# Norm squares moved from VectorE to ScalarE over two slots, and every second round of V's transposed tiles copied by ScalarE

## The reference, cut to what matters

```python
q = z @ wq @ fcq_w + fcq_b          # attention A: through 64 columns, with biases
k = z @ wk @ fck_w + fck_b
v = z @ wv @ fcv_w + fcv_b
...
qkv = jnp.einsum('bnc,cd->bnd', x, w_qkv)        # attention B: one dense projection
...
scores = q @ k.T / 8;  attn = softmax(scores);  out = (attn @ v) @ w_out + b_out   # 16 heads of 64
...
h = jax.nn.gelu(x @ w1 + b1, approximate=False);  out = h @ w2 + b2                # 4096 wide
```

## Time and profile before

| quantity | value |
|---|---|
| median of the two timed runs | 3740.32 us |
| the two runs | 3833.94 and 3646.69 us |
| the profiled execution, its own time | 3663.36 us |
| its span (first to last instruction, slowest core) | 3662.3 us |
| spans of the eight cores | 3630.1 to 3662.3 us |
| busy: TensorE, ScalarE, VectorE | 2674.0, 1453.9, 1224.7 us |
| mean granted TensorE clock, cores | 0.854 to 0.869 |

### The profile page before, as it was taken

The page is one execution under the profiler, slowest core; times in us unless marked ns, Lnnn a source line. Parts: engine busy times, 40 slices in busy tenths (PEclk is TensorE's granted clock), DMA queues, the critical chain, the costliest instruction groups (busy, mean ns, idle before and its releaser), DMA issues.

```text
span 3662.3 us, 33549 instructions; the slowest of 8 cores (3630.1 to 3662.3 us)
## 1 busy us (share of the span) xinstructions
PE 2674.0 (73%) x10664; PEld 924.1 (25%) x10664; DVE 1224.7 (33%) x1874; ACT 1453.9 (40%) x1496; POOL 64.8 (2%) x122
## 2 busy tenths in 40 slices
PE   5444878587875577989847658786778765789997
PEld 1110222122222233434313212222122222334333
DVE  4554344434444021120253334444343430212200
ACT  2112989488950202112200009892689601021120
POOL 0000000000000000000000000000000000000000
PEclk9655999789988789999967779998899987899788
DMA  3000000000004715133011110001000038151332
GB/s 104 0 0 6 4 4 4 3 3 5 4 9 62 133 24 92 35 58 69 1 18 18 18 23 4 4 5 26 2 5 4 7 50 140 32 92 35 58 69 92
DMA packets 32806, 121.00 MB, mean 33 GB/s; under 512 B 7552, under 2 KB 11648, under 8 KB 22400
## 3 DMA queue, kind: packets, MB, share of 16 engines
q0 software_dynamic: 20832, 97.53, 15.4%
q1 hardware_dynamic: 11808, 21.32, 1.9%
HBM read 203.50 MB, written 8.39 MB: 58 GB/s over the span
## 4 chain that ended last, share of the span: by engine, by line
PE 51%; ACT 17%; DVE 14%; DMA 7%; issue 6%; another core or an unknown queue 2%; DVEq 1%; SPq 0%; ACTq 0%; POOLq 0%; POOL 0%
ACT POOL L430 14%; DMA POOL<-w_h 5%; PE PS_A L619 5%; DVE POOL L138 5%; PE PS_B L619 5%; PE PS_A L589 5%; PE PS_B L589 4%; PE PS_A L369 3%; PE PS_D L619 3%; PE PS_C L444 3%; DVE SCR L138 3%; PE PS_D L444 2%; DVE sstat L138 2%; PE PS_B L369 2%
## 5 line engine op out<-in xcount | busy, mean ns | idle before, releaser
L430 ACT ACTIVATE POOL<-PS_A,ebias 128x1024 bf16<-128x1024 f32 x512 | 571.0, 1115 | 345.3 <-PE PS_A L374 296.2
L430 ACT ACTIVATE POOL<-PS_B,ebias 128x1024 bf16<-128x1024 f32 x512 | 571.3, 1116 | 32.0 <-PE PS_C L448 13.2
L589 PE MATMUL PS_A<-BIG,POOL 128*128 128x512 bf16 x1024 | 260.6, 401 | 146.7 <-DMA POOL<-w_h 139.4
L369 PE MATMUL PS_A<-BIG,POOL 64*128 64x512 bf16 x512 | 198.1, 387 | 94.0 <-ACT POOL L430 89.8
L142 ACT ACT_TABLE_LOAD x16 | 20.5, 1283 | 613.3 <-PE PS_A L589 518.8
L589 PE MATMUL PS_B<-BIG,POOL 128*128 128x512 bf16 x1024 | 252.6, 391 | 0.0
L369 PE MATMUL PS_B<-BIG,POOL 64*128 64x512 bf16 x512 | 197.9, 387 | 70.9 <-ACT POOL L430 68.1
L138 DVE RECIPROCAL PF<-SCR 33x512 f32<-33x512 f32 x64 | 214.1, 3345 | 65.8 <-DMA SCR<-PF 65.8
L444 PE MATMUL PS_C<-POOL 128*65 128x512 bf16 x512 | 214.8, 420 | 0.0
L444 PE MATMUL PS_D<-POOL 128*65 128x512 bf16 x512 | 206.8, 404 | 6.1 <-ACT POOL L430 6.1
L619 PE MATMUL PS_A<-BIG,POOL 128*128 128x512 bf16 x768 | 188.3, 408 | 28.7 <-DVE BIG L138 26.5
(11 more groups left out here) (139 smaller groups left out, 3013.2 us busy)
## 6 DMA issues: line engine op xcount, KB each, us to landing
POOL<-w_h POOLq DMA_DIRECT2D x64, 1024.0 KB, 8.5
POOL<-w_h POOLq DMA_DIRECT2D x2, 8192.0 KB, 55.1
X<-xT SPq DMA_DIRECT2D x8, 1024.0 KB, 23.2
yT<-X SPq DMA_DIRECT2D x8, 1024.0 KB, 12.2
BIG<-POOL SPq DMA_DIRECT2D x64, 64.0 KB, 1.9
POOL<-wqkv_kv POOLq DMA_DIRECT2D x16, 256.0 KB, 4.3
POOL<-wqkv_q POOLq DMA_DIRECT2D x16, 256.0 KB, 3.5
POOL<-fco_h POOLq DMA_DIRECT2D x8, 256.0 KB, 4.3
```

The costliest lines, as they stand in the source:

```text
L369: nc.tensor.matmul(PSx[:, 0:512], lt0, rh0, start=True, stop=True, tile_position=(0, 0))
L430: nc.scalar.activation(psb, PSx[:, :], AF.Exp, bias=ebias[:, c:c + 1], scale=0.125),
L589: tt = nc.tensor.matmul(PSx[:, ucoff:ucoff + 512], wg[:, dc * 512 + j * 128: dc * 512 + j * 128 + 128], BIG2[:, hoff(dc):hoff(dc) + 512], ...
```

## The change

emit_knorm and emit_qnorm2_and_ebias: the squares are made by ScalarE (Square), in two SBUF buffers in turn; their column sums go to PS_D and PS_E in turn; the row maxima stay on VectorE. The square of slice i waits for the matmul of slice i-2, and the matmul of slice i for the square of slice i and the maximum of slice i-2. On entry ScalarE waits once for everything that TensorE and VectorE have been given so far.

emit_vtranspose: the copies of rounds 1 and 3 are made by ScalarE (Identity), those of rounds 0 and 2 by VectorE as before. Round 3 of the transposes therefore waits for ScalarE, round 2 for VectorE.

Nothing is added to or taken from the number of matmuls, maxima, copies or DMAs; 128 squares and 128 tile copies change engine.

```diff
@@ emit_vtranspose
-                    p.wait(nc.tensor, "dve", round_ev[r4 - 2])
+                    p.wait(nc.tensor, round_eng[r4 - 2], round_ev[r4 - 2])
...
-                p.wait(nc.vector, "te", t)
+                if r4 % 2 == 0:
+                    p.wait(nc.vector, "te", t)
+                else:
+                    p.wait(nc.scalar, "te", t)
...
+                    if r4 % 2 == 0:
+                        v = vop("tensor_copy", da, sa)
+                    else:
+                        v = sop("activation", da, sa, AF.Identity)
                 round_ev[r4] = v
+                round_eng[r4] = "dve" if r4 % 2 == 0 else "act"
@@ emit_knorm
+            p.wait(nc.scalar, "te")
+            p.wait(nc.scalar, "dve")
+            psl = [PS_D[0:1, 0:512], PS_E[0:1, 0:512]]
...
-                p.wait(nc.vector, "te")
-                v = vop("tensor_mul", ksq, kc_ap, kc_ap)
-                p.wait(nc.tensor, "dve", v)
-                t = p.inc(nc.tensor.matmul(PS_D[0:1, 0:512], ones_b[:, 0:1], ksq,
-                                           start=True, stop=True), "te", 1)
-                p.wait(nc.vector, "te", t)
-                vop("reduce_max", S_KSL(sl), PS_D[0:1, 0:512], axis=AX.X)
+                if sl >= 2:
+                    p.wait(nc.scalar, "te", tmm[sl - 2])
+                sq = sop("activation", ksq, kc_ap, AF.Square)
+                p.wait(nc.tensor, "act", sq)
+                if sl >= 2:
+                    p.wait(nc.tensor, "dve", mx[sl - 2])
+                tmm[sl] = p.inc(nc.tensor.matmul(psl[sl % 2], ones_b[:, 0:1],
+                                                 ksq, start=True, stop=True),
+                                "te", 1)
+                p.wait(nc.vector, "te", tmm[sl])
+                mx[sl] = vop("reduce_max", S_KSL(sl), psl[sl % 2], axis=AX.X)
```

More of the change, by code:

```diff
@@ L292, in emit_vtranspose @@
             round_ev = {}
+            round_eng = {}
             for r4 in range(4):
@@ L307, in emit_vtranspose @@
                                P_VAR + kt * VSTR + 132 * cpair + 132]
-                    v = vop("tensor_copy",
-                            dst.rearrange("p (h f) -> p h f", h=2)[:, :, 0:64],
-                            psv.rearrange("p (h f) -> p h f", h=2))
+                    da = dst.rearrange("p (h f) -> p h f", h=2)[:, :, 0:64]
+                    sa = psv.rearrange("p (h f) -> p h f", h=2)
+                    if r4 % 2 == 0:
+                        v = vop("tensor_copy", da, sa)
+                    else:
+                        v = sop("activation", da, sa, AF.Identity)
@@ L311, in emit_vtranspose @@
                 round_ev[r4] = v
+                round_eng[r4] = "dve" if r4 % 2 == 0 else "act"
             return p.cnt["dve"]
         def emit_knorm(cpair, sq_off):
+            p.wait(nc.scalar, "te")
+            p.wait(nc.scalar, "dve")
+            psl = [PS_D[0:1, 0:512], PS_E[0:1, 0:512]]
+            tmm = {}
+            mx = {}
             for sl in range(4):
-                ksq = POOL[:, sq_off:sq_off + 512]
+                ksq = POOL[:, (sq_off if sl % 2 == 0 else MB + 8192):
+                           (sq_off if sl % 2 == 0 else MB + 8192) + 512]
@@ L325, in emit_knorm @@
             vop("reduce_max", S_KMAX(cpair), sstat[0:1, 16:20], axis=AX.X)
         def emit_qnorm2_and_ebias(sq_off):
+            p.wait(nc.scalar, "te")
+            p.wait(nc.scalar, "dve")
+            psl = [PS_D[0:1, 0:512], PS_E[0:1, 0:512]]
+            tmm = {}
+            mx = {}
             for c in range(NPAIR):
                 for qqi in range(2):
-                    qsq = POOL[:, sq_off:sq_off + 512]
+                    gi = c * 2 + qqi
+                    qsq = POOL[:, (sq_off if gi % 2 == 0 else MB + 8192):
+                               (sq_off if gi % 2 == 0 else MB + 8192) + 512]
@@ L331, in emit_qnorm2_and_ebias @@
                     q_ap = BIG2[:, qqi * 4096 + c * 512: qqi * 4096 + c * 512 + 512]
[L332 to L339, removed]
+                    if gi >= 2:
+                        p.wait(nc.scalar, "te", tmm[gi - 2])
@@ new lines, in emit_qnorm2_and_ebias @@
+                    sq = sop("activation", qsq, q_ap, AF.Square)
+                    p.wait(nc.tensor, "act", sq)
+                    if gi >= 2:
+                        p.wait(nc.tensor, "dve", mx[gi - 2])
+                    tmm[gi] = p.inc(nc.tensor.matmul(psl[gi % 2], ones_b[:, 0:1],
+                                                     qsq, start=True, stop=True),
+                                    "te", 1)
+                    p.wait(nc.vector, "te", tmm[gi])
+                    mx[gi] = vop("reduce_max", sstat[0:1, 20 + qqi:21 + qqi],
+                                 psl[gi % 2], axis=AX.X)
```

## The result

The changed kernel takes 3497.6 us in the median of 11 runs, against 3685.2 for the kernel before in 10 runs beside it. The medians take in runs that one die lengthened; the ratio is made from undisturbed runs alone: 0.957, 95% interval 0.9535 to 0.960, so 4.3% faster. Against the profiled execution of before (3663.4) that is 159 us; 153 was forecast. The profiled execution of the changed kernel took 3510.87 us, with a span of 3509.8 on its slowest core, core 6.

A forecast was written before the change was run, and what follows sets the result against it. No single engine bounds the kernel; stages are serial chains through several engines. Savings of 45 (A's K/V stage), 28 (B's) and 80 us (Q norms) sum to 153, taking 3663.4 to 3510 us; range 3475 to 3563.

The forecast's parts named there:

- The chain in A's K/V stage: Attention A's K/V stage, timed step by step from the last K eviction: 5.6 us saved a pair, 45 us in all.
- The two new ones: ScalarE's new instructions: 0.63 us for a 128x512 square, 0.28 for a 128x128 copy (bounds 0.21 and 0.60).
- The Q norms: Four Q norm blocks: VectorE sets the pace at 1.80 us per two slices, 20 us saved a block, 80 in all.
- The other two cycles: Q norms: maximum, matmul, maximum over one slot 1.59 us; square, matmul, square 1.52; both under VectorE's 1.80 a pair.
- B's K/V stage: Attention B's K/V stage: transposes 5.63 us after the last V matmul, 3.5 us saved a pair, 28 in all.
- The gap that stood for all: B's K/V stage: one gap, last V matmul to next K matmuls, 12.4 us before, counted for all pairs.
- the rival of the higher clock: B's K/V stage: the shorter gap may keep TensorE's higher clock, 10 us; with A's part 3492 us, chance 0.13.
- Higher clock in A's stage: Attention A's K/V stage: five chain matmuls a pair at 0.38 us, not 0.58, give 8 us; higher-clock rival's chance 0.13.
- ScalarE slower than its rows: Copies of 0.60 us and squares of 1.12 leave 119 of the 153 us: 3544 us, chance 0.14.
- No overlap: Norms: each square still waits for the maximum before it, 2.37 us a slice against 2.11: 3675 us, chance 0.02.
- Slower dense matmuls: The ffn, B's and output projection matmuls run at the last ffn's slower pace: up to 3744 us, chance 0.05.

The follow-up runs named there:

- run 4: The changed kernel with one square buffer and one PSUM bank, waiting on the slice just before: 3574 us, 0.9784 of the kernel before.
- copies alone: The kernel before with only the copies of transposed rounds 1 and 3 moved to ScalarE: 3633 us, 0.9957 of the kernel before.
- K norms alone: The kernel before with only emit_knorm taken from the changed kernel: 0.9844 of the kernel before, 57 us less.
- run 5: The changed kernel with the squares back on VectorE, two buffers, two banks and code order kept: 0.9962 of the kernel before.
- run 6: The changed kernel with squares on VectorE, the next slice's square issued ahead of the maximum: 0.968 of the kernel before, 116 us less.

## Why the prediction was right

**The chain in A's K/V stage.** Every term stood within 0.03 us, as the rows above show, and the stage gave 45.3 of 45 us. It could be exact because nearly every term was a hand-over or a duration of this trace. The two new ones, 0.63 for the square and 0.28 for the small copy, measured 0.631 and 0.278. The 0.28 was a choice: it rests on 0.83 ns a column, which no row of the kernel before shows; the difference of rows, at 1.01, would have given 0.21. With the new row the choice is borne out: (598 - 278) / 384 = 0.83 ns a column.

**The Q norms.** VectorE sets the pace at 1.81 us a pair of slices; four blocks gave 79.6 of 80. The other two cycles were shorter, as worked out: run 4, which takes the second slot away, brings out the cycle over one bank at 1.61 us (1.59 in the working).

**B's K/V stage, sized too small.** 34.4 us measured on core 1 against 28, and so 159 against 153 in all. The timeline of the changed kernel on core 1:

```profile
1902.54 1.89 PE L816 MATMUL PS_B<-BIG,POOL 128*128 128x512 bf16 x8
...
1905.27 2.80 ACT L142 ACTIVATE POOL<-POOL 128x512 bf16<-128x512 bf16 x4
...
1909.72 0.14 DVE L138 TENSOR_REDUCE sstat<-sstat 1x1 f32<-1x4 f32 x1
1910.12 1.01 PE L302 MATMUL PS_C<-identb_s,POOL 128*128 128x128 bf16 x8 [1.42 <-DVE sstat L138]
...
1913.20 2.34 PE L816 MATMUL PS_A<-BIG,POOL 128*128 128x512 bf16 x5
```

The last V matmul ends at 1904.43, and transposes start 5.69 later (5.63 in the working), the next K matmuls 8.77 later where before they started 1999.16 - 1986.96 = 12.20 later: 3.4 of the 3.5 us. What the sum left out shows when the stage is split into its eight runs of 64 matmuls and the eight gaps behind them (from the end of a pair's last V matmul to the next matmul of a projection). In us, means of the six cores of each kernel whose traces have all 512 matmuls of this stage:

| B's K/V stage | before | copies alone | K norms alone | one slot (run 4) | the change |
|---|---|---|---|---|---|
| one of the first seven gaps | 12.55 | 11.64 | 9.61 | 11.00 | 8.82 |
| the last gap | 14.92 | 12.92 | 11.91 | 12.13 | 10.02 |
| eight gaps | 102.8 | 94.4 | 79.2 | 89.1 | 71.8 |
| eight runs of matmuls | 126.4 | 126.0 | 128.0 | 130.6 | 122.4 |

On core 1 the gaps gave 30.9 us of the 34.4 and the runs 3.5. The surplus of 6.4 us over the forecast has three parts. The gap that stood for all (12.20) was among the shortest of the first seven, which go from 12.2 to 12.8: 1.6 us. The last gap, which I took as the others, shrank by 4.8 us and not 3.5: 1.3. And the runs of matmuls became shorter, which I had left out of the sum: 3.5.

In those runs TensorE reached its upper level (2.4 GHz) sooner: the first eight K matmuls after a gap take 2.99 to 3.43 us on this core, mean 3.12, and took 3.02 to 3.62 before, mean 3.42. The mean granted clock over the stage rose from 0.78 to 0.84, in part only because less of the stage is gap. That was the rival of the higher clock, priced at 1.4 us a pair; it came true in part, at some 0.4 us a pair. That the shorter gap is its cause is not shown. In the table the runs do not follow the gaps: with gaps of 9.61 us (127.7 to 128.6 on the six cores) and of 11.00 (129.1 to 131.5) they took longer than before (125.9 to 127.0). What decides when the level comes back stays open.

**The rivals.** *Higher clock in A's stage:* did not happen, 0.51 before and after. *ScalarE slower than its rows:* excluded by the two durations. *No overlap:* excluded: two slices take 1.81 us where it asked for 4.74. Run 5 shows a chain that does not overlap, at 2.22 us a slice. *Slower dense matmuls:* they did not slow down more than before. The last ffn by stretch, first of the kernel before on core 1, its slowest:

```profile
3058.00:3662.00 604.00, 514.94 (x2108) 215.09 (x2108) 81.88 (x133) 101.25 (x141) 16.28 (x30) 0.87 0.33 68
```

then of the changed kernel, core 6 (its slowest) and core 1:

```profile
2908.00:3509.00 601.00, 506.71 (x2066) 213.44 (x2106) 81.88 (x133) 101.03 (x141) 16.35 (x30) 0.88 0.34 68
```

```profile
2895.00:3475.00 580.00, 483.78 (x2108) 207.93 (x2108) 81.90 (x133) 101.24 (x141) 16.18 (x30) 0.93 0.35 71
```

The slowest core's last ffn takes 604 and 601 us at 0.87 and 0.88; another core of the same execution needs 580 at 0.93. This stage scatters by some 30 us from core to core with the granted clock in both kernels (577 to 609 us before, 576 to 603 now), and the change moves neither end.
**How exact the number is.** The forecast of 3510 us and the 3510.87 of the profiled execution agree by some luck. The stages gave 6 us more than forecast, and this execution is the slowest of those behind the ratio (the fastest took 3475.28): its cores 6 and 7 spent over 20 us more in the last ffn than the other six. The fair comparison is 159 us against 153.

## What to carry to other kernels

When a stage goes square, matmul, maximum over three engines, add up its possible cycles (each engine's own work, and each round trip over one buffer) and change what sets the longest: here both were needed, since a second bank and buffer are worth nothing while one engine makes the square and the maximum in that order (run 5), and the second engine with one of each has only half of the gain (run 4). Look at the order of the code first: issuing the next square ahead of the maximum gave, with the copies, nearly three quarters of the gain while the squares stayed on VectorE (run 6). Read the whole stage and not one pair: the gap that was taken for all eight cost the forecast 3 us. A chain that has been made short is still a chain in front of the next stage; placing it between the projections' matmuls took another 2.6%.

## What the runs showed that was not expected

The sum of eight gaps and the length of the matmuls between them do not move together in B's K/V stage: the runs of matmuls took 122.4 us in the changed kernel and 130.6 with one slot, on either side of the 126.4 before, with gaps that were shorter than before in both.

In run 5 the first two slices of each stretch of norms have one wait in front of the matmul (for the square), the later ones a second (for VectorE's maximum two slices back, long since reached). From core 4, slices 1 and 2 of a Q block:

```profile
694.72 0.42 DVE L138 TENSOR_TENSOR POOL<-BIG 128x512 bf16<-128x512 bf16 x1
695.29 0.58 PE L361 MATMUL PS_E<-POOL,ones_b 128*1 128x512 bf16 x1 [1.53 <-DVE POOL L138]
...
697.08 0.43 DVE L138 TENSOR_TENSOR POOL<-BIG 128x512 bf16<-128x512 bf16 x1
697.75 0.58 PE L361 MATMUL PS_D<-POOL,ones_b 128*1 128x512 bf16 x1 [1.88 <-DVE POOL L138]
```

The matmul with one wait starts 0.15 us after the end of its square, the one with two 0.25 (0.24 by the rounded rows). Over the eight cores it is 0.14 to 0.15 for all 320 matmuls with one wait and 0.25 or more for all 704 with two (median 0.25); in run 6 the same counts give the same figures, and in the kernel before, where every such matmul has one wait, all 1024 have 0.14 to 0.15. The bank is not the reason, as slice 1 already goes to the other one. So a second wait costs 0.1 us here even when it is already fulfilled, and on a chain this adds up: 14 of 16 slices in a Q block, some 1.4 us.
